# Cross-attention with batches b and b+2 in one block: the output product in 128x128 tiles, and a new written order

## The reference

```python
x = _layernorm(x + attn(x))            # linear attention, 16 heads, features exp(q wq_feat), exp(k wk_feat)
x = _layernorm(x + xattn(x, ctx))      # softmax cross-attention, 16 heads of 8, output product with Wo
x = _layernorm(x + ffn(x))             # ternary W_fc (128 to 512), gelu, layer norm with ln_w, ln_b, ternary W_proj

# xattn: the part that the change touches
Q, K, V = proj(query, Wq, bq), proj(key, Wk, bk), proj(value, Wv, bv)
scores = jnp.einsum('bhqd,bhkd->bhqk', Q, K) * sm_scale
attn = jax.nn.softmax(scores, axis=-1)
ctx = jnp.einsum('bhqk,bhkd->bhqd', attn, V)
ctx = ctx.transpose(0, 2, 1, 3).reshape(B, S, D)
out = jnp.einsum('bsd,ed->bse', ctx, Wo) + bo
```

## Time and profile before

| | before |
|---|---|
| median of the runs | 727.86 us |
| time of the profiled execution | 724.73 us |
| span of its trace | 722.8 us |
| PE busy | 672.4 us, 93% |
| DVE busy | 534.2 us, 74% |
| ACT busy | 460.0 us, 64% |
| POOL busy | 422.8 us, 58% |
| granted PE clock | full for 35 of 40 slices, lower in the last five |

### The profile page before, as it was taken

How to read it: one execution, slowest core, us unless ns; L and a number is a source line. 1 busy time by engine, 2 the same in 40 slices (tenths; PEclk the granted TensorE clock), 3 DMA queues, 4 the chain that set the end, 5 groups by cost and what they waited for, 6 DMA issues and landing times.

```text
span 722.8 us, 31396 instructions
## 1 busy us (share of the span) xinstructions
PE 672.4 (93%) x13629; PEld 477.2 (66%) x13629; DVE 534.2 (74%) x1475; ACT 460.0 (64%) x799; POOL 422.8 (58%) x469
## 2 busy tenths in 40 slices
PE   7999999999999999999999999999999999894664
PEld 6776766667676776676676676677676675573453
DVE  2555666787877878787878778687887777966857
ACT  3546566849494867859394867759484859464432
POOL 4032224858485776858485766858485767555433
PEclk9999999999999999999999999999999999996986
DMA  8002121343526252533424262622325142412110
GB/s 319 16 17 61 18 61 33 63 82 57 102 46 105 48 115 51 96 56 61 90 51 102 47 120 47 99 54 65 87 61 101 37 90 47 91 18 59 32 30 30
DMA packets 119995, 49.97 MB, mean 69 GB/s; under 512 B 110513, under 2 KB 110770, under 8 KB 119730
## 3 DMA queue, kind: packets, MB, share of 16 engines
q1 hardware_dynamic: 119858, 47.96, 32.5%
HBM read 17.01 MB, written 4.19 MB: 29 GB/s over the span
## 4 chain that ended last, share of the span: by engine, by line
PE 57%; POOL 11%; ACT 11%; DVE 9%; issue 7%; DMA 5%; SPq 1%; POOLq 0%; DVEq 0%; ACTq 0%
PE bank L333 7%; PE bank L316 6%; PE bank L306 6%; POOL gall L1047 5%; PE bank L382 4%; DMA cT<-cs 4%; ACT PT L631 3%; PE bank L445 3%; PE bank L409 2%; PE bank L480 2%; PE bank L256 2%; PE bank L424 2%; PE bank L329 2%; DVE st L841 2%; PE bank L481 2%
## 5 line engine op out<-in xcount | busy, mean ns | idle before, releaser
L316 PE MATMUL bank<-Mh,GT 128*32 128x128 f32 x4096 | 122.8, 273 | 0.2
L316 PEld LDWEIGHTS bank<-Mh,GT 128*32 128x32 f32 x4096 | 110.4, 110 | 18.3 <-issue 10.2
L1047 POOL TENSOR_TENSOR gall<-gall,lnr 128x512 f32<-128x512 f32 x56 | 71.7, 1292 | 35.1 <-DVE st L841 35.1
L871 DVE TENSOR_REDUCE mx<-bank 128x8 f32<-128x512 f32 x128 | 78.1, 680 | 11.2 <-PE bank L382 11.2
L1052 POOL TENSOR_TENSOR gs<-gall,gs 128x512 f16<-128x512 f32 x56 | 65.1, 1162 | 7.9 <-ACT gs L678 7.9
L306 PE MATMUL bank<-kp,xs 64*128 64x512 f32 x256 | 68.9, 627 | 0.3 <-issue 0.3
L1005 POOL TENSOR_TENSOR rstd<-ve,mhalf 128x4 f32<-128x4 f32 x64 | 64.9, 1015 | 5.3
L631 ACT ACTIVATE PT<-bank 128x512 f32<-128x512 f32 x128 | 64.4, 627 | 5.6 <-PE bank L409 5.5
L333 PE MATMUL bank<-Cb,qT 128*64 128x128 f32 x1024 | 66.8, 273 | 0.0
L1002 POOL TENSOR_SCALAR ve<-mv 128x4 f32<-128x4 f32 x64 | 12.5, 196 | 92.2 <-DVE mv L848 88.9
L814 DVE TENSOR_TENSOR qT<-qT,bank 128x512 f32<-128x512 f32 x64 | 39.7, 681 | 34.2 <-PE bank L299 34.2
(11 more groups left out here) (172 smaller groups left out, 1712.6 us busy)
## 6 DMA issues: line engine op xcount, KB each, us to landing
cxT<-in_cxT SPq DMA_DIRECT2D x16, 256.0 KB, 4.0
...
Qm<-in_Wvp SPq DMA_DIRECT2D x1, 1024.0 KB, 7.3
gT<-gs SPq DMA_TRANSPOSE x56, 3.1
...
```

What stands on the lines that cost most here:

```text
L316: m = e.matmul(bk[32 * j:32 * j + 32, tile(g_)], GT[b % 4][:, tile(hh, 32)], Mh[:, tile(hh)], start=True, stop=True)
L871: e.tensor_reduce(mx[s % 2][:, c0:c0 + 8], bank[uses["score", s, i][0]][:, :].rearrange("p (n k) -> p n k", k=64), AX.X, ALU.max).then_inc ...
L1047: e.tensor_tensor(g[t][:, :], g[t][:, :], lnr[:, :], ALU.mult).then_inc(s_gs, 1)
```

## The change

The batches that share a block of scores become b and b+2 in place of b and b+1: the context is laid out so on the host (`cxT`), Q is taken from the other batch, and `pv` writes its columns in the order that makes the turned context of one batch a full tile of 128 features. With that `proj` is six matmuls of 128x128 per `tp` in place of 24 of 64x128, `oturn` is one product of 128x256 on DVE in place of two of 128x128, and Wo needs no second copy (one DMA of 128 KB less, `wo` on 128 columns, at the end of HEAD). The score, prob and pv steps have as many instructions as before, of the same size.

The three tables of the order are all new. In PERIOD two more copies of `c` and one of `pv` are on DVE in place of ACT. In HEAD the loads come in another order: Wvp (1024 KB) now stands ahead of xT of group 0, and the first cxT is last.

```diff
 HEAD = """
-wb zeros small1 wk WkT wq k0@0 mh0 g0+@0 xq g1+@0 mh1 k1@0 WqT loadc@0 k2@0 k3@0 bias2 q0@0 nbeta q1@0 q2@0 q3@0 gam ks+@0 split@0 g2+@0 g3+@0 g4@0
+small1 wb wk wq k0@0 xq k1@0 k2@0 WkT nbeta q0@0 WqT k3@0 Wvp zeros gam q1@0 bias2 loadx@0 ks+@0 small2 q2@0 q3@0 kst@0 biasA g0@0 g1@0 bv mh0 split@0
...
 PERIOD = """
...
-oturn0@2 oturn1@2 gs3@3 qproj@1 cs0@2 cs1@2 kproj@1 vproj@1 g6 g7 dT c4+ c5 c6+ c7+ loadx@-2 split@-1 bc0 loadc bc1 bc2 gl2@3 bc3 proj0@2 proj1@2 st2@2
+oturn1@2 gh0@3 cs1@2 gh1@3 q3 kst g4 g5 g6 g7 qproj@1 kproj@1 c2+ gs2@3 c3+ dT c4 c5 gs3@3 c6 c7+ gl2@3 bc0 bc1 gl3@3 bc2 bc3 gh2@3 gh3@3 proj0@2
...
-        cs, xWoh, xWol = [sb(f"cs{i}", 512, F16) for i in two], sb("xWoh", 256, F16), sb("xWol", 256, F16)
-        xWo2 = PT[1][:, 0:256]
+        cs, xWoh, xWol = [sb(f"cs{i}", 512, F16) for i in two], sb("xWoh", 128, F16), sb("xWol", 128, F16)
...
# score (prob likewise)
-                            b = 4 * tp + 2 * t2 + bb
+                            b, k = 4 * tp + 2 * bb + t2, 4 * tp + 2 * t2 + bb
                             m = e.matmul(bk[64 * bb:64 * bb + 64, tile(t2, 256)], Qu[rows, tile(b, 64)],
-                                         Kg[rows, :].rearrange(by_head, g=4)[:, :, tile(b, 64)], start=True, stop=True)
+                                         Kg[rows, :].rearrange(by_head, g=4)[:, :, tile(k, 64)], start=True, stop=True)
...
# pv
-                        m = e.matmul(bk[32 * j:32 * j + 32, tile(4 * t2 + g_, 64)], V3[s % 2][:, 32 * tp + 16 * t2 + hh, :], PT[tp][:, c0:c0 + 64],
+                        m = e.matmul(bk[32 * j:32 * j + 32, tile(2 * g_ + t2, 64)], V3[s % 2][:, 32 * tp + 16 * t2 + hh, :], PT[tp][:, c0:c0 + 64],
...
# proj
-                for t2 in two:
-                    for a_ in two:
-                        for W, lo in ((xWoh, 0), (xWoh, 1), (xWol, 0)):
-                            for bb in two:
-                                r = slice(64 * bb, 64 * bb + 64)
-                                c0 = 256 * lo + 128 * t2 + 64 * a_
-                                m = e.matmul(bk[r, tile(t2)], cT[tp][r, c0:c0 + 64], W[r, tile(a_)], start=(a_ == 0 and W is xWoh and lo == 0), stop=(a_ == 1 and W is xWol))
+                for bb in two:
+                    e.matmul(bk[:, tile(bb)], cT[tp][:, tile(bb)], xWoh[:, :], start=True, stop=False)
+                    e.matmul(bk[:, tile(bb)], cT[tp][:, tile(2 + bb)], xWoh[:, :], start=False, stop=False)
+                    m = e.matmul(bk[:, tile(bb)], cT[tp][:, tile(bb)], xWol[:, :], start=False, stop=True)
...
# oturn on DVE
-                for t2 in two:
-                    own = b3[:, 8 * t2:8 * t2 + 8, 0:18].rearrange("p h (b c) -> p h b c", b=2)[:, :, :, 0:8]
-                    m = e.tensor_tensor(to[:, t2], own, r4[:, t2].unsqueeze(3).to_broadcast([128, 8, 2, 8]), ALU.mult)
-                m.then_inc(emptied("oturn", s, tp)[0], 1)
+                own = b3[:, :, 0:18].rearrange("p m (b c) -> p m b c", b=2)[:, :, :, 0:8]
+                e.tensor_tensor(to, own, r3.unsqueeze(3).to_broadcast([128, 16, 2, 8]), ALU.mult).then_inc(emptied("oturn", s, tp)[0], 1)
...
-                    e.dma_start(xWo2, a["xWo2"]).then_inc(s_Wo2, 16)
...
-    A["cxT"] = w["ctx_1024"].reshape(NG, 512, D).transpose(0, 2, 1)
+    A["cxT"] = w["ctx_1024"].reshape(NG, 2, 2, 2, T, D).transpose(0, 5, 1, 3, 2, 4).reshape(NG, D, 512)
```

More of the change, by code:

```diff
@@ L37 @@
+sbar loadc@0 wo
 """
 PERIOD = """
-k0 k1 k2 score0@2 score1@2 o0@1 o1@1 o2@1 o3@1 rows@2 g0+ ap2@3 st1@1 g1 g2 g3+ down0@4 k3 q0 q1 down1@4 ap1@1 down2@4 q2 down3@4 xb x1s@1 st3@4 ab2@3
-prob0@2 ap3@4 prob1@2 ab1@1 up0@3 up1@3 up2@3 gs0@3 up3@3 gs1@3 c0+ c1 stat@3 c2+ pv0@2 gh0@3 ks c3 pv1+@2 g4+ g5 q3 kst gl0@3 gs2@3 gh1@3 gl1@3
-oturn0@2 oturn1@2 gs3@3 qproj@1 cs0@2 cs1@2 kproj@1 vproj@1 g6 g7 dT c4+ c5 c6+ c7+ loadx@-2 split@-1 bc0 loadc bc1 bc2 gl2@3 bc3 proj0@2 proj1@2 st2@2
-gh2@3 gl3@3 gh3@3
+k0 k1 down0@4 down1@4 k2 score0@2 split@-1 score1@2 o0@1 o1@1 o2@1 o3@1 rows@2 st1@1 ap2@3 g0+ g1+ g2 g3+ down2@4 down3@4 q0 k3 st3@4 ab2@3 q1 xb
@@ L43 @@
+prob0@2 ap1@1 prob1@2 x1s@1 ab1@1 ap3@4 c0 ks pv0@2 gs0@3 c1 loadx@-2 pv1@2 gs1@3 stat@3 up0@3 gl0@3 up1@3 loadc gl1@3 up2@3 up3@3 oturn0@2 q2 cs0@2
+oturn1@2 gh0@3 cs1@2 gh1@3 q3 kst g4 g5 g6 g7 qproj@1 kproj@1 c2+ gs2@3 c3+ dT c4 c5 gs3@3 c6 c7+ gl2@3 bc0 bc1 gl3@3 bc2 bc3 gh2@3 gh3@3 proj0@2
+vproj@1 proj1@2 st2@2
 """
 TAIL = """
-k0@1 k1@1 vproj@2 score0@3 k2@1 ap2@4 score1@3 loadc@1 o0@2 o1@2 o2@2 o3@2 xb@1 rows@3 st1@2 ab2@4 gs0@4 k3@1 q0@1 q1@1 up0@4 up1@4 down0@5 gs1@4
-down1@5 up2@4 x1s@2 ap1@2 up3@4 down2@5 down3@5 g0@1 prob0@3 stat@4 ab1@2 st3@5 gl0@4 prob1@3 c0@1 kproj@2 pv0@3 ks+@1 pv1@3 g1@1 gs2@4 gh0@4 g2@1
@@ L47 @@
[L47 to L50, removed]
@@ new lines @@
+c2@1 c3+@1 pv1+@3 q0@1 oturn0@3 oturn1@3 gh2@4 gs3@4 kst@1 cs0@3 score0@2 cs1@3 vproj@2 score1@2 gh3@4 q1@1 q2@1 q3@1 proj0@3 proj1@3 down0@4 gl2@4
+gl3@4 rows@2 xb@1 st2@3 ab1@2 g6+@1 ap3@5 g7+@1 dT@1 down1@4 down2@4 down3@4 st3@4 prob0@2 prob1@2 c4+@1 c5+@1 ap2@3 ab2@3 c6+@1 gs0@3 gs1@3 c7+@1
+bc0@1 bc1@1 bc2@1 bc3@1 pv0@2 stat@3 up0@3 up1@3 up2@3 pv1+@2 up3@3 oturn0@2 oturn1@2 o0@1 cs0@2 o1@1 o2@1 cs1@2 o3@1 kproj@1 st1@1 gh0@3 gl0@3 ap1@1
+proj0@2 proj1@2 flip+@1 st2@2 ab2@2 ap2@2 gs2@3 gl1@3 gs3@3 gh1@3 qproj@1 flip3@2 vproj@1 gh2@3 score0@1 gl2@3 ab1@1 up0@2 gh3@3 score1@1 up1@2 down0@3
@@ L53 @@
+down1@3 rows@1 gl3@3 down2@3 ap3@4 up2@2 up3@2 prob0@1 down3@3 st3@3 prob1@1 pv0+@1 pv1+@1 cs0@1 cs1@1 stat@2 oturn0@1 oturn1@1 ap3@3 proj0@1 proj1@1
+st2@1 turn0@2 turn1@2 turn2@2 turn3@2 ab2@1 ap2@1 down0@2 down1@2 flip3@1 down2@2 down3@2 st3@2 stat@1 up0@1 up1@1 up2@1 up3@1 turn0@1 turn1@1 turn2@1
 turn3@1 ap3@2 down0@1 down1@1 down2@1 down3@1 st3@1 ap3@1
@@ L644, in wo @@
             def wo():
-                w.wait_ge(s_Wo2, 16)
-                e.activation(xWoh[:, :], xWo2, ACT.Copy).then_inc(s_woh, 1)
+                w.wait_ge(s_small2, 16)
+                e.activation(xWoh[:, :], xWo[:, :], ACT.Copy).then_inc(s_woh, 1)
             def flip3(s):
@@ L783, in wo @@
                 w.wait_ge(s_woh, 1)
[L784 to L785 removed]
+                w.wait_ge(s_small2, 16)
+                e.tensor_tensor(xWol[:, :], xWo[:, :], xWoh[:, :], ALU.subtract).then_inc(s_wol, 1)
             def ksum_turn(s):
```

26 lines of the change are left out of this document (10 added, 16 removed).

## The result

| | before | after |
|---|---|---|
| median of 20 runs each, us | 728.04 | 734.27 |
| ratio after/before, 95% interval | | 1.0065 [1.0045, 1.0084] |
| profiled execution (its span), us | 724.73 (722.8) | 734.98 (733.2) |
| start of the third score step, us | 145.2 | 146.9 |
| 11 periods from there, us | 443.7 (40.34 each) | 466.3 (42.39 each) |

The ratio leaves out three of the 20 runs after (738.0, 738.3 and 742.9 us), which count as slow runs; with them the medians are 0.86% apart.

The account below looks back on a forecast made before the run. PE was taken as the bound through most of the run, the last group's dependent chain at the end; -11.2 -3.5 +0.5 -5.0 = -19.2, so 724.7 - 19.2 + 3.1 = 708.6 us (702 to 714).

Parts of the forecast that it names:

- A: Output product on PE: six wide matmuls save 0.35 us per step over 32 steps, -11.2 us (-10.5 to -11.9).
- Rival 3: Output product: weight loads paid in the open, 0.6 us more per step, so 728, no change; chance 0.04.
- B: Period: PE idle falls from 0.69 to 0.4 us despite small waits at Dblk, -3.5 us (-8.3 to +4).
- rival 1: Period: late Dblk chain or context transposes queued behind the cxT load idle PE 0.7 us more, 717; chance 0.24.
- Rival 2: Period: DVE ahead of `stat` becomes the bound, 1.6 us or more per period, slower; chance 0.08 including bad head and tail.
- C: Head: 768 KB more loaded ahead of the split on POOL, +0.5 us (0 to +1.7).
- D: Tail: shorter last-group chain as DVE applies stop waiting beside POOL, less a later flip, -5.0 us (-8 to +3).
- -1.4 for its products: Tail: the last two output product steps, in the open chain at lower clock, lose half of 2.73 us.
- The own apply: Tail: the last group's own output apply on DVE falls from 4.65 to about 2.0 us, -2.6.
- The apply put back: Tail: an earlier group's output apply between the last `o` additions leaves the chain, -3.6 us; putting it back restores that.

Follow-up runs that it names:

- e12: The kernel of experiment 3 with the next group's first k moved from the head of the period to ahead of the first output product: 701.75 us, ratio 0.9653.
- e1: The changed kernel's code with all three order tables (HEAD, PERIOD, TAIL) of the kernel before: 721.60 us, ratio 0.9932.
- experiments 2 and 3: Two successive PERIOD edits of the changed kernel: cxT load issued ahead of the x loads (718.27 us), then also the `up` products earlier (707.11 us).
- experiment 3: The changed kernel with early cxT load, plus `up` ahead of `c1` and `pv1`, statistics between those, one `pv` copy back on ACT: 707.11 us, ratio 0.9753.
- e2: The changed kernel with the PERIOD table of the kernel before; HEAD and TAIL stay new: 707.66 us, ratio 0.9729.
- e11: e2 with the new TAIL only up to the last group's last `o` addition, the remaining steps in the old TAIL's order: 714.56 us, ratio 0.9816.

## Why the prediction was wrong, step by step

- **Output product (A, -11.2): right in its mechanism, too small in size.** Six rows per step, 0.055 us apart at the full clock, as `down` had it: 675.00, 675.05, 675.11. In the 11 periods of e12 `proj` is 11.2 us shorter, where I had 7.7 for those 22 steps. A step now takes 0.34 us, as forecast; but the old one took 0.80 to the next step (17.5 us over 22, without 1.0 of waits), and I had counted its four blocks alone (0.68). So the product gives 0.46 per step, not 0.35. Rival 3, the weight loads in the open, is out. The Trainium skill (TensorE: Matmul & The Clock Gate, Part 3) says that a weight load overlaps running matmuls only when the row group differs, which would speak for that rival. This trace does not agree with it for full tiles: the products run 0.055 us apart, while one of their weight loads is shown at 96 ns, so the loads do overlap. But a product saved is a period saved only if the next wait has slack: e1 kept 3.5 of some 10.
- **Idle time of the period (B, -3.5): wrong; this step failed.** It said that POOL's chain to Dblk "can begin when `up`, the gelu and the first statistics are through, some 1.6 us after `up` begins (a product 0.4, an activation 0.6, 0.6 of DVE)". It began after 3.4 (377.53 to 380.91). The 1.6 left out ACT's table load of 1.28 us (the profile of before has it too, right behind the exponentials), and the parts that it did count took 0.5 more: 0.7 until both matmuls of the first `up` are out, 0.6 for the activation, 0.8 for the statistics. The chain itself took the 12.4 that I worked out (380.91 to 393.33). So up to Dblk it was 15.8 us, not 14.0, against my 14.4 to 14.9 of work on PE: the slack was not there. Nor did PE pay where I looked: it waited for Dblk 2.5 us in six waits, and the time went to cT and to the bank of `g`, by the next two points. The ends of B, -8.3 to +4, were drawn from PE's idle time alone; the 11 periods came to +33.5 against forecast. Of these, 26.4 go with the two edits of experiments 2 and 3 (466.3 to 439.9); the other 7 lie mostly at `bc` and `c` and were not traced further.
- **What I saw as a rival and priced too low: the cxT load on SP** (rival 1, "0.7 us more per period", 717). It is the larger half: 1.6 to 1.8% (12 to 13 us) against 1.4 to 1.5% for the late `up`, by `bc` and, three times, by the slow clock. I did not count SP's queue: 2.8 us of gelu transposes, 0.5 of load and 2.6 of context, whose four inputs POOL made within 2.5 us (the first low part at 388.7, the last at 391.1).
- **What I did not see at all: the bank of `g`.** `cn` stands behind `stat` in DVE's row, and the last of `g` needs the bank that `cn` empties. 9.9 us, and experiment 3 takes it away. The step that I moved (`up`) had two followers on two engines, and I followed only POOL's.
- **Rival 2 (DVE as the bound, +1.6 per period): wrong in its mechanism, near in its time, and that by luck.** DVE waits before `stat` for ACT (1.81 us); it is not full at 33.75 of 42.39.
- **Head (C, +0.5): about right.** The split began at 9.50 in place of 7.79, as the load order made it, and the first product at 11.87 for 11.63. The third score came 1.7 us later, but that is the periods ahead of it: in e2, with the new HEAD and the old PERIOD, it stands at 145.2, as before. So the new HEAD cost nothing.
- **Tail (D, -5.0 and -1.4 for its products): too small.** 11.3 us went behind the last `o`. The own apply lost 3.5 (I had 2.6). The apply put back costs 0.8 us by the medians and 3.1 in the profiled runs, where I had 3.6; four runs do not settle it. e11 shows 8 us from the order behind the last `o` as a whole, of which the own apply is the largest single piece that I can name. The 5.5 us ahead of it (e1 to e2, 62.5 to 57.0 from the end of the 11 periods to the end of the last `o`) I had as an end of the range only.

The sum against the profiled span: forecast 703.6, measured 733.2, 29.6 over: periods +33.5, head +1.2, the rest -5.1.
